# Attention: query scores and all that follows one round later behind the DMA transpose; the values copied two rounds behind the spread

## The reference, cut to what matters

```python
def _L1_attn_ref(x, Wk, Wq, Wv, Wp, bp):     # x: 32 x 1024 x 96
    H = 6; hs = C // H                       # 6 heads of 16
    k = (x @ Wk).reshape(B, H, T, hs)
    q = (x @ Wq).reshape(B, H, T, hs)
    v = (x @ Wv).reshape(B, H, T, hs)
    wei = jnp.einsum('bhtd,bhsd->bhts', q, k) * C ** (-0.5)
    wei = jnp.where(tril(ones(T, T)), wei, -jnp.inf)
    wei = jax.nn.softmax(wei, axis=-1)
    out = jnp.einsum('bhts,bhsd->bhtd', wei, v).reshape(B, T, C)
    return out @ Wp + bp
```

## Time and profile before

| | us |
|---|---|
| median of 3 runs | 2781.7 |
| lowest and highest run | 2777.81, 2783.16 |
| the profiled execution, its time | 2775.24 |
| the profiled execution, first to last instruction (span) | 2773.5 |

### The profile page before, as it was taken

One profiled execution on the slowest core, in us unless ns is written; L12 is line 12 of the kernel. 1 busy time (PEld: TensorE's weight loads), 2 busy tenths in 40 slices (PEclk: granted clock), 3 DMA queues, 4 the chain that ended last, 5 costly groups with the idle time before them and its releaser, 6 DMA issues. The chain is left out here.

```text
span 2773.5 us, 83152 instructions
## 1 busy us (share of the span) xinstructions
PE 2537.8 (92%) x29309; PEld 1507.9 (54%) x29309; DVE 2111.7 (76%) x3025; ACT 1966.0 (71%) x3751; POOL 1509.3 (54%) x2545
## 2 busy tenths in 40 slices
PE   4999999999999868999999999999999996899996
PEld 2555555555555435555555555555555553455553
DVE  3576666666666357888888888888888884678997
ACT  2677778787877536777777777777777773677775
POOL 0142433333333347777887878777878772224445
PEclk9999999999999969999999999999999998999998
DMA  1122223232323256566666666666666644335545
GB/s 36 40 75 75 97 68 102 68 102 68 102 68 97 74 114 104 115 116 119 122 122 116 122 122 120 116 124 121 117 118 123 123 92 118 88 110 143 146 132 160
DMA packets 777486, 290.84 MB, mean 105 GB/s; under 512 B 702866, under 2 KB 760499, under 8 KB 777395
## 3 DMA queue, kind: packets, MB, share of 16 engines
q1 hardware_dynamic: 776050, 288.43, 45.3%
q10 hardware_dynamic: 1344, 1.18, 0.1%
HBM read 100.77 MB, written 87.29 MB: 68 GB/s over the span
## 5 line engine op out<-in xcount | busy, mean ns | idle before, releaser
L1031 DVE TENSOR_REDUCE at_row_max<-at_ps_queries 128x1 f32<-128x1024 f32 (+7 forms) x1536 | 1075.6, 747 | 159.4 <-PE at_ps_queries L914 159.2
L987 ACT ACTIVATE at_probs<-at_ps_keys 128x512 f32<-128x512 f32 x1344 | 730.4, 596 | 288.4 <-PE at_ps_keys L929 287.3
L904 PE MATMUL at_ps_queries<-at_turned 48*128 48x512 f16 (+3 forms) x2304 | 611.6, 333 | 116.9 <-DMA at_turned<-at_spread 94.8
L929 PE MATMUL at_ps_keys<-at_turned 50*128 50x128 f16 (+3 forms) x3456 | 577.6, 275 | 6.1 <-ACT at_diag_probs L987 0.5
L949 PE MATMUL at_ps_values<-at_probs,at_v 128*32 128x128 f32 x10752 | 417.5, 280 | 0.5 <-DVE at_out L1023 0.4
L929 PEld LDWEIGHTS at_ps_keys<-at_turned 50*128 50x128 f16 x3456 | 231.9, 94 | 198.0 <-ACT at_probs L987 67.0
L851 POOL TENSOR_TENSOR at_recip<-at_out,at_minus_one 128x8 f32<-128x8 f32 x192 | 313.8, 1634 | 2.8 <-DVE at_out L1023 2.8
L949 PEld LDWEIGHTS at_ps_values<-at_probs,at_v 128*32 128x32 f32 x10752 | 261.4, 110 | 92.2 <-issue 73.3
L513 POOL TENSOR_TENSOR cb_o_hat<-cb_o,cb_o_scale 128x768 f32<-128x768 f32 x32 | 48.0, 1501 | 459.8 <-DVE cb_o_scale L433 459.8
L904 PEld LDWEIGHTS at_ps_queries<-at_turned 48*128 48x128 f16 x2304 | 171.1, 94 | 174.5 <-DVE at_row_max L1031 129.8
L987 ACT ACTIVATE at_diag_probs<-at_ps_keys 128x512 f32<-128x512 f32 x384 | 230.8, 601 | 37.4 <-PE at_ps_keys L929 24.0
(11 more groups left out here) (223 smaller groups left out, 5080.4 us busy)
## 6 DMA issues: line engine op xcount, KB each, us to landing
qkv_rows<-cb_packed SPq DMA_DIRECT2D x32, 1152.0 KB, 7.6
at_stacks<-qkv_rows SPq DMA_DIRECT2D x192, 192.0 KB, 2.8
cb_x<-in_x_dram SPq DMA_DIRECT2D x32, 384.0 KB, 3.7
cb_x_again<-in_x_dram SPq DMA_DIRECT2D x32, 384.0 KB, 4.5
x_after_conv<-cb_x SPq DMA_DIRECT2D x32, 384.0 KB, 5.1
ff_att_rows<-attention_rows SPq DMA_DIRECT2D x32, 384.0 KB, 4.3
ff_x<-x_after_conv SPq DMA_DIRECT2D x128, 96.0 KB, 2.3
x_after_attention<-ff_x SPq DMA_DIRECT2D x30, 384.0 KB, 3.0
```

The costliest lines, as they stand in the source:

```text
L904: mm = pe.matmul(scores[:, c0:c0 + width], QT[Q_ROWS, slot, qb * P:(qb + 1) * P], KT[Q_ROWS, slot, k0 * P:k1 * P], start=(c0 == 0), stop=True,
L929: mm = pe.matmul(pk[:, bank_k, c0:c0 + n * P], KT[K_ROWS, slot, kb * P:(kb + 1) * P], QT[K_ROWS, slot, q0 * P:(q0 + n) * P], start=(c0 == ...
L987: act.activation(probs, pk[:, ring(r, u + (u > MAX_TURN)), :], ACT.Exp, scale=scale).then_inc(S["probs"], 1)
L1031: ins = dve.tensor_reduce(MX[:, r % 2, qb:qb + 1], pq[:, (NR * r + g) % QBUFS, b0 * P:(b0 + n) * P], AX.X, ALU.max)
```

## The change

The reader of the transposed tile, TensorE's query scores, moves from round h+2 to round h+3, and everything that follows it moves by one round too: row maxima, their split, turn, copy and DMA, key scores, exponentials, mask, values, output and stores. The load, the spread and the transpose keep their rounds. The copy of the values into V (L862) moves from round h to h+2, since V has six slots and the values are read in round h+6 now; its wait for the slot and its place in GpSimd's list (behind the waits for the loaded rows, ahead of the spread copies) stay. The stores fall into odd rounds instead of even ones. No instruction is added or removed, and the pipeline has one round more.

```diff
-    VALUES_BACK = 5
+    VALUES_BACK = 6
@@ SP
-                    if on(3):
-                        q = (r - 3) % SLOTS
-                        sp.wait_ge(S["max_copied"], i - 2)
+                    if on(4):
+                        q = (r - 4) % SLOTS
+                        sp.wait_ge(S["max_copied"], i - 3)
                         sp.dma_start(QT[MAX_ROWS, q, :], MT[:, q % 2, :]).then_inc(max_in[q], 16)
-                    if on(7) and r % PAIR == 0:
-                        q, b = (r - 8) % SLOTS, lap + (r - 8) // SLOTS
-                        sp.wait_ge(S["out_ready"], i - 6)
+                    if on(8) and r % PAIR == 1:
+                        q, b = (r - 9) % SLOTS, lap + (r - 9) // SLOTS
+                        sp.wait_ge(S["out_ready"], i - 7)
...
-                _pipeline(sp, body, NHEADS, 8, SLOTS, ahead=1)
+                _pipeline(sp, body, NHEADS, 9, SLOTS, ahead=1)
@@ GpSimd
-                    if on(3):
-                        slot = (r - 3) % 2
-                        pool.wait_ge(S["row_max"], NR * (i - 2))
-                        _above(pool.wait_ge, S["max_turned"], i - 4)
+                    if on(4):
+                        slot = (r - 4) % 2
+                        pool.wait_ge(S["row_max"], NR * (i - 3))
+                        _above(pool.wait_ge, S["max_turned"], i - 5)
...
                     if on(0):
                         pool.wait_ge(loaded[r], _dmas(lap, r, 0, SLOTS))
-                        _above(pool.wait_ge, S["values"], NU * (i - SLOTS + 1))
                         _above(pool.wait_ge, turned_in[r], _dmas(lap, r, SLOTS, SLOTS))
-                        v = ST[:, r, :, PW:PW + HD].bitcast(FP32)
-                        pool.tensor_tensor(V[:, r, :, 0:HD], v, ONE[:, :, :].broadcast_to([P, TILES, HD]), ALU.mult)
+                    if on(2):
+                        q = (r - 2) % SLOTS
+                        _above(pool.wait_ge, S["values"], NU * (i - 2 - SLOTS + 1))
+                        v = ST[:, q, :, PW:PW + HD].bitcast(FP32)
+                        pool.tensor_tensor(V[:, q, :, 0:HD], v, ONE[:, :, :].broadcast_to([P, TILES, HD]), ALU.mult)
+                    if on(0):
                         h = HD // 2
...
@@ TensorE
-                    slot, g = (r - 2) % SLOTS, u // 2
+                    slot, g = (r - 3) % SLOTS, u // 2
                     if u == 0:
-                        pe.wait_ge(turned_in[slot], _dmas(lap, r, 2, SLOTS))
+                        pe.wait_ge(turned_in[slot], _dmas(lap, r, 3, SLOTS))
...
-                        back, k = 3 - (u - LAG) // NU, (u - LAG) % NU
+                        back, k = 4 - (u - LAG) // NU, (u - LAG) % NU
                         if on(back):
-                            key_scores(i - back, (r - back) % SLOTS, _dmas(lap, r, back, SLOTS), i, r, u, k, on(3))
-                        if on(2):
-                            query_scores(i - 2, r, lap, u)
-                        if u == MAX_TURN and on(3):
+                            key_scores(i - back, (r - back) % SLOTS, _dmas(lap, r, back, SLOTS), i, r, u, k, on(4))
+                        if on(3):
+                            query_scores(i - 3, r, lap, u)
+                        if u == MAX_TURN and on(4):
                             turn_max(i, r)
```

More of the change, by code:

```diff
@@ L879, in body @@
                                            ).then_inc(S["masked"], 1)
-                _pipeline(pool, body, NHEADS, 7, SLOTS)
+                _pipeline(pool, body, NHEADS, 9, SLOTS)
             @block.tensor
@@ L884, in turn_max @@
                 def turn_max(i, r):
-                    back, k = 3 - (MAX_TURN - LAG) // NU, (MAX_TURN - LAG) % NU
-                    pe.wait_ge(S["max_parts"], i - 2)
+                    back, k = 4 - (MAX_TURN - LAG) // NU, (MAX_TURN - LAG) % NU
+                    pe.wait_ge(S["max_parts"], i - 3)
                     _above(pe.wait_ge, S["probs"], NU * (i - back) + k - 1)
                     row = pk[:, ring(r, MAX_TURN + 1), 0:P // 2].bitcast(FP16)
-                    pe.transpose(row, MP[:, (r - 3) % 2, :], w["ident_hf"][:, :]).then_inc(S["max_turned"], 1)
+                    pe.transpose(row, MP[:, (r - 4) % 2, :], w["ident_hf"][:, :]).then_inc(S["max_turned"], 1)
                 def query_scores(h, r, lap, u):
-                    slot, g = (r - 2) % SLOTS, u // 2
+                    slot, g = (r - 3) % SLOTS, u // 2
                     if u == 0:
-                        pe.wait_ge(turned_in[slot], _dmas(lap, r, 2, SLOTS))
+                        pe.wait_ge(turned_in[slot], _dmas(lap, r, 3, SLOTS))
                     if u % 2 == 0:
                         _above(pe.wait_ge, S["row_max"], NR * h + g - QBUFS + 1)
-                    scores = pq[:, (NR * r + g) % QBUFS, u % 2 * BANK:(u % 2 + 1) * BANK]
+                    scores = pq[:, (NR * (r - 1) + g) % QBUFS, u % 2 * BANK:(u % 2 + 1) * BANK]
                     c0 = 0
@@ L988, in body @@
                                            scale=scale).then_inc(S["probs"], 1)
-                        if u == MAX_TURN and on(3):
-                            act.wait_ge(S["max_turned"], i - 2)
-                            _above(act.wait_ge, max_in[(r - 5) % SLOTS], _dmas(lap, r, 5, SLOTS))
+                        if u == MAX_TURN and on(4):
+                            act.wait_ge(S["max_turned"], i - 3)
+                            _above(act.wait_ge, max_in[(r - 6) % SLOTS], _dmas(lap, r, 6, SLOTS))
                             row = pk[:, ring(r, MAX_TURN + 1), 0:P // 2].bitcast(FP16)
-                            act.activation(MT[:, (r - 3) % 2, :], row[0:2 * TILES, :], ACT.Copy
+                            act.activation(MT[:, (r - 4) % 2, :], row[0:2 * TILES, :], ACT.Copy
                                            ).then_inc(S["max_copied"], 1)
-                _pipeline(act, body, NHEADS, 8, SLOTS)
+                _pipeline(act, body, NHEADS, 9, SLOTS)
             @block.vector
@@ L1018, in body @@
                     for g, region in enumerate(REGIONS):
[L1019 to L1022, removed]
+                        if g == NR - 1 and on(6):
+                            q = (r - 6) % 2
+                            dve.wait_ge(S["values"], NU * (i - 5))
+                            _above(dve.wait_ge, S["out_ready"], i - 7)
                             dve.transpose(OUT[:, q, :, :].rearrange("p t d -> p (t d)"),
@@ L1025, in body @@
                                           ).then_inc(S["out_turned"], 1)
[L1026 to L1027 removed]
+                        if on(3):
+                            dve.wait_ge(S["q_scores"], NR * (i - 3) + g + 1)
                             if g == 0:
[L1029 removed]
+                                _above(dve.wait_ge, S["max_parts"], i - 4)
                             for qb, b0, n in region:
[L1031 to L1032 removed]
+                                ins = dve.tensor_reduce(MX[:, (r - 3) % 2, qb:qb + 1],
+                                                        pq[:, (NR * (r - 1) + g) % QBUFS, b0 * P:(b0 + n) * P], AX.X, ALU.max)
                             ins.then_inc(S["row_max"], 1)
[L1034 removed]
+                _pipeline(dve, body, NHEADS, 9, SLOTS)
 def project_and_ffn(nc, w, att, x1, x2, y_out):
```

22 lines of the change are left out of this document (11 added, 11 removed).

## The result

The changed kernel takes 2714.3 us (median of four runs, 2710.1 to 2716.9) against 2781.7 before (median of three); the ratio is 0.976, with a 95% interval of 0.974 to 0.978. That is 67 us less (61 to 73). Forecast were 2719 in the median, and 2712.7 against the profiled execution, whose successor took 2713.15.

What follows compares the result with a forecast made beforehand. TensorE and VectorE, near full, wait on each other, and TensorE on a late DMA transpose every second round. 2775.24 less 62.5 gives 2712.7 profiled; from the runs' median 2719.2, so 2719 us, range 2709 to 2740.

Steps and rivals of the forecast that it cites:

- Step 1: TensorE's query scores: the transpose's lateness of 0.64 us becomes 5.7 us of reserve, so the wait goes entirely.
- Step 2: Attention loop: without the wait every round takes 6.32 us, at most 6.36, against 6.668 on average; 62.5 us less.
- The second road: Second estimate of the gain: TensorE's 72.6 us of transpose waits in 90 rounds, less 0.18 each for VectorE: 56.4 us.
- Step 3: GpSimd's copy of the values (0.40 us), two heads later at the same place, never blocks and costs nothing.
- Step 4: Ends of the attention stage: the extra round lies in front, where TensorE has nothing; 0 taken, at most 6.4 us.
- Step 5: SP's queue: 11.40 us of unbroken issue fits a 12.64 us pair of rounds, keeping 1.2 us of reserve.
- rival B: SP's issue becomes the bound, taking from the gain above 12.64 us per pair; about 2885 us, chance 0.04.
- Rival A: The maxima's DMA becomes TensorE's key-score wait if landing exceeds 3.0 us; at 3.3, 2748 us; chance 0.06.
- Rival C: No change, 2781 us: VectorE hides the wait, short rounds repay long, or the transpose's issue slides along; chance 0.05.

Runs made afterwards that it cites:

- the run without the reserve: The changed kernel with the DMA transpose also issued one round later, so its reader gains no extra round: 2789.5 us, ratio 1.004.

## Why the prediction was right

**Step 1, the wait goes.** Right, by the tile's own view and by the run without the reserve, which brings it back. That the cause is the order in SP's queue was argued from two timelines; the stores moved behind the transpose prove it.

**Step 2, the size.** 62.5 us forecast, 62.8 measured between first and last copy. The short round of 6.32 us stands for the rounds of the loop, but for one in each pass of six: 6.36, which the prediction had read from peeled rounds, comes back there, 29 times for 1.1 us in all. Against that the second interval between copies, which the sum kept as it was, went from 9.55 to 8.51 us. That the two cancel, and leave the forecast within 0.3 us, is luck. The long first-pass rounds went with their low clock: from 1080 to 1130 us the granted clock is 1.00 where it was 0.83 before. The median fell by 67, but with an interval of 61 to 73 that is no disagreement. The second road, waits less 0.18 each, gave 56.4 and was the poorer: it misses what the long waits cost beyond themselves. The first fourteen intervals between VectorE's turns, up to 1134 us, took 105.9 us before and 88.8 after, 17.1 less, where five waits had made up 11.5.

**Step 3, the values' copy.** Free, as said, by two runs. What the prediction did not see is that leaving it in round h would have been nearly free as well: 3.5 us more, with SP waiting as long as now, for the spread.

**Step 4, the added round.** Nothing: from the first query matmul to the last turn of the output the stage takes 1295 us before and 1232 after, 63 less, as between the copies of the maxima.

**Step 5 and rival B, SP's reserve.** 1.2 us per pair forecast, 1.06 measured. With 0.8 more of issue the loop hardly changes (one round of many passes by up to 0.2 us), with 2.4 more SP is the bound. The rival's mechanism is real, and its point of decision, 12.64 us of issue per pair, lies between the two; the change alone doesn't reach it.

**Rival A, the maxima's DMA.** Its landing was put at 1.8 us and is 2.0; its room was put at 3.0 us and is 2.92. In the kernel after, SP's issue behind a transpose and the key scores that need it:

```profile
1509.05 0.68 SPq L809 DMA_DIRECT2D at_turned<-at_max_rows  x1
...
1511.97 0.22 PE L932 MATMUL at_ps_keys<-at_turned 50*128 50x128 f16 x1
...
1080.00:1130.00 50.00, 48.52 (x903) 30.71 (x903) 46.06 (x72) 38.91 (x80) 41.47 (x96) 1.00 0.69 130
```

It stays 0.9 clear, and is the first to go once SP is loaded. (The last row is the window of the loop's first pass that step 2 speaks of.)

**Rival C** is out: VectorE did not hide the wait, and short rounds did not repay long ones, since all rounds of the loop are 6.32 to 6.37 us now.

**What was wrong** came behind the prediction: that VectorE and TensorE bind the round in turns along one loop, and that any 0.3 us taken from it would count. There are two loops.

## What to carry to other kernels

When an engine waits every second time, look for what its supplier's queue does every second time. Here five small stores, 2.4 us of issue that nobody waits for, stood ahead of a transpose that everybody waited for; either more depth or a better order cures it, and the order needs no slot for longer. Before taking work off a ring of two engines, list every loop that a buffer's release closes: a cut in one of two equal loops brings next to nothing.

## What the runs showed of the hardware

Waits of TensorE of about 0.7 us (1.04 at the most), one per 13 us, left its clock at 2.4 GHz from 1130 us on in the kernel before. With waits lengthened to 1.4 us in the median (1.8 at the most), one per 14 us, it fell to 1.2 GHz in many stretches, and a lateness of 68 us cost 106. It doesn't fall behind each of them: behind one of 1.65 us the granted clock of the next 5 us was 0.70, but two thirds of the long rounds kept their 7.6 us. The Trainium skill (TensorE: Matmul & The Clock Gate, HAM oscillation) describes a kernel whose clock falls back at its wait for DMA on every tile; the steady waits of the kernel before did not show it, the lengthened ones do in part of the rounds.

A DMA of 4 KB between two tiles of SBUF took 2.0 us from issue to use, right behind a transpose on the same queue (1504.72 to 1506.72 in the run with two more DMAs); the spare ones, not directly behind a transpose, landed in 1.7 in the median. Each such DMA cost SP some 0.6 to 0.7 us of issue, plus 0.1 to 0.3 before the next.
